# Two layers of attention and expert FFN on one core: who combines the expert results between the layers, and in which order the second layer's projections run

## The reference, cut to what matters

```python
x = x + _L0_xattn_ref(_layernorm(x), ctx_1024, ctx_1024, ...)   # 16 heads of 16, windows of 128 tokens
x = x + _L0_ffn_ref(_layernorm(x), ...)                         # 16 experts, 2 per token, and a shared one
x = x + _L1_xattn_ref(_layernorm(x), ctx_1024, ...)             # 16 heads of 16, 256 keys per query
x = x + _L1_ffn_ref(_layernorm(x), ...)                         # 8 experts, 2 per token

def _L0_ffn_ref(x, ...):
    logits = x @ router_w.T
    top_vals, top_idx = top_k(logits, 2)
    gates = sigmoid(top_vals)
    ...                              # every token: gates[0]*y_first + gates[1]*y_second + shared

def _L1_xattn_ref(q, kv, ...):
    qh, kh, vh = q @ Wq + bq, kv @ Wk + bk, kv @ Wv + bv
    attn = softmax(qh @ kh.T / sqrt(16))
    return (attn @ vh) @ Wo + bo
```

## Time and profile before

| | us |
|---|---|
| median of 3 runs | 889.52 (887.65 to 891.84) |
| the profiled execution | 891.48 |
| its span, first to last instruction | 889.7 |
| PE busy | 799.2 (90%) |
| DVE busy | 593.7 (67%) |
| ACT busy | 394.5 (44%) |
| GpSimd busy | 239.6 (27%) |

### The profile page before, as it was taken

The page is one execution under the profiler, slowest core; times in us unless marked ns, Lnnn a source line. Parts: engine busy times, 40 slices in busy tenths (PEclk is TensorE's granted clock), DMA queues, the critical chain, the costliest instruction groups (busy, mean ns, idle before and its releaser), DMA issues.

```text
span 889.7 us, 23526 instructions
## 1 busy us (share of the span) xinstructions
PE 799.2 (90%) x8688; PEld 595.3 (67%) x8689; DVE 593.7 (67%) x1394; ACT 394.5 (44%) x767; POOL 239.6 (27%) x201
## 2 busy tenths in 40 slices
PE   7998999898978888788979999989998999999993
PEld 4555666565667666666634666657487999999993
DVE  3456787789936555555966888856878755555552
ACT  3344556553412222223422666765776444444440
POOL 0004000100026666662003000001045644444442
PEclk8999999999989999999999999999999999999998
DMA  9886312234452222225845433128247333343331
GB/s 278 141 104 72 98 38 74 95 125 132 136 188 78 83 83 83 77 89 149 166 50 71 74 121 121 50 73 308 60 140 196 65 71 68 67 69 64 67 61 25
DMA packets 72345, 91.41 MB, mean 103 GB/s; under 512 B 14705, under 2 KB 57713, under 8 KB 72273
## 3 DMA queue, kind: packets, MB, share of 16 engines
q1 hardware_dynamic: 58112, 62.19, 29.3%
q0 software_dynamic: 13728, 27.94, 12.5%
q10 hardware_dynamic: 432, 0.26, 0.1%
HBM read 60.86 MB, written 17.56 MB: 88 GB/s over the span
## 4 chain that ended last, share of the span: by engine, by line
PE 62%; DVE 16%; issue 8%; ACT 5%; DMA 4%; another core or an unknown queue 2%; DVEq 1%; POOL 0%; SPq 0%; POOLq 0%; ACTq 0%
PE bank L1024 13%; PE bank L1011 12%; PE bank L763 5%; PE bank L783 3%; PE bank L918 3%; PE bank L729 3%; PE bank L578 3%; PE bank L609 3%; PE bank L559 2%; PE bank L930 2%; DMA out<-arena,put_i 2%; PE bank L996 2%; PE bank L596 2%; DVE arena L1850 2%
## 5 line engine op out<-in xcount | busy, mean ns | idle before, releaser
L1024 PE MATMUL bank<-arena 128*128 x1218 | 281.2, 274 | 6.8 <-DVE arena L1863 2.9
L1399 ACT ACTIVATE arena<-bank,router_b 128x128 f32<-128x128 f32 x312 | 87.4, 373 | 112.1 <-DMA router_b<-in_exp_b 97.3
L1556 DVE TENSOR_REDUCE neg_max<-bank 128x2 f32<-128x512 f32 (+1 forms) x180 | 117.3, 684 | 27.8 <-PE bank L729 27.5
L1024 PEld LDWEIGHTS bank<-arena 128*128 128x128 f16 x1218 | 119.2, 98 | 19.3 <-issue 17.3
L1011 PE MATMUL bank<-att,arena 128*128 128x128 f16 x960 | 106.2, 221 | 0.3 <-issue 0.3
L1237 ACT ACTIVATE arena<-bank 128x1024 f32<-128x1024 f32 x96 | 96.4, 1024 | 11.3 <-PE bank L748 11.2
L1011 PE MATMUL bank<-arena 128*128 128x128 f16 x1128 | 97.8, 223 | 2.4 <-issue 2.4
L1011 PE MATMUL bank<-attT,arena 128*128 128x128 f16 x912 | 99.3, 219 | 0.0
L1011 PEld LDWEIGHTS bank<-att,arena 128*128 x960 | 92.6, 99 | 6.4 <-issue 0.5
L2018 POOL DMA_INDIRECT out<-arena,put_i x39 | 67.3, 1725 | 107.4 <-DVE arena L1876 85.9
L1011 PEld LDWEIGHTS bank<-attT,arena 128*128 x912 | 86.6, 98 | 5.5
(11 more groups left out here) (223 smaller groups left out, 1349.4 us busy)
## 6 DMA issues: line engine op xcount, KB each, us to landing
arena<-arena SPq DMA_DIRECT2D x96, 128.0 KB, 5.2
arena<-in_exp_up SPq DMA_DIRECT2D x16, 512.0 KB, 3.9
arena<-in_exp_b SPq DMA_DIRECT2D x39, 128.0 KB
arena<-in_ctxT SPq DMA_DIRECT2D x8, 512.0 KB, 7.2
arena<-in_exp_dn SPq DMA_DIRECT2D x16, 256.0 KB, 4.2
xn_d<-arena POOLq DMA_DIRECT2D x8, 512.0 KB, 4.6
arena<-y_d SPq DMA_DIRECT2D x8, 512.0 KB, 8.9
arena<-in_exp_dn SPq DMA_DIRECT2D x4, 1024.0 KB, 5.5
```

Of the source, the lines that this page charges most:

```text
L1024: last = mm(yP[u], hidT[u][x][:, k], weights(e, 1, w, k * D, D), start=n == 0, stop=n == n_second - 1)
L1399: last = fn(hid[:, k * P:(k + 1) * P], upP[u][:, half, (k % 4) * P:(k % 4 + 1) * P], ACT.Relu, bias=b1_col[u][:, k:k + 1], scale=1 / WS)
L1556: v.tensor_reduce(neg_max[u][:, column(m * HM):column(m * HM) + 2 * HM - 1:2], mx[m % 2].rearrange("p (h k) -> p h k", h=HM), AX.X, ALU.ma ...
```

## The change

Five things, all in layer 1:

1. Chunks 2 and 3 are combined by GpSimd (`combine_late`): one product of 128x2048 numbers with the gates and two sums of 128x1024 for each chunk. DVE combines chunks 0 and 1 as before. GpSimd's bias sums no longer wait for all queries.
2. The keys of chunk 1 go to the bank `trT`, and so need no wait for the keys of chunk 0. The order of the products on PE, of the copies on ACT and of the steps on DVE is rewritten.
3. The eight first maxima follow directly behind the last turned chunk. The queries of chunk 3 are multiplied in four pieces between them (`last_queries`).
4. The values of chunk 3 are multiplied in four pieces between the maxima of tile 1 (`last_values`).
5. SP issues the stack DMAs of keys in another place: chunk 1's ahead of the load of the last expert results, chunks 2 and 3 inside `project`.

```diff
+        keysP = [[kP] * NC, [kP, trT, kP, kP]]
+        LATE = 2
...
@@ SP, project(1)
                     keys(1, 0)
                     load_results(2)
+                    keys(1, 1)
                     load_results(3)
-                    keys(1, 1)
+                    keys(1, 2)
                     queries(1, 0)
+                    keys(1, 3)
                     queries(1, 1)
+                    queries(1, 2)
...
@@ PE, keys, turn_tokens
-                    after(pe, s["kparts_ready"], c)
+                    if l == 0 or c > 1:
+                        after(pe, s["kparts_ready"], c - 1 if l and c == 2 else c)
...
+                    if l and c == 0:
+                        pe.wait_ge(s["kparts_ready"], 2)
...
@@ PE, project(1)
                     project_bias()
+                    keys(1)
                     pe.wait_ge(B[0]["y_ready"], NS[0])
                     values(0)
-                    keys(1)
+                    keys(2)
                     values(1)
-                    keys(2)
                     turn_tokens(0, 0)
-                    values(2)
                     queries(0, 0)
                     keys(3)
                     turn_tokens(1, 1)
-                    values(3)
+                    values(2)
                     queries(1, 1)
                     turn_tokens(2, 0)
                     queries(2, 0)
                     turn_tokens(3, 1)
-                    first_maxima(l, 0, 2)
-                    queries(NC - 1, 1)
-                    first_maxima(l, 2, 8)
+                    first_maxima(l, 0, 8)
                     turn_first(l)
...
+            def last_queries(n):
+                s, (m, k) = B[1], (n // KD, n % KD)
+                if n == 0:
+                    pe.wait_ge(s["qparts_ready"], NC - 1)
+                last = mm(qP[:, m], wqk[1][:, 0, k, m * P:(m + 1) * P], xnT[(NC - 1) % 2][:, k], start=k == 0, stop=k == KD - 1)
...
+            def last_values(t):
+                for k in range(KD):
+                    last = mm(vP[...], ctxT[...], wv[:, k], start=k == 0, stop=k == KD - 1)
...
@@ PE, first_maxima
-                    if l and m >= 2:
-                        if m == 2:
-                            pe.wait_ge(s["v_ready"], NC)
-                        keep_running(spare, 5 if m == 2 else 1, 3 * P if m == 2 else 2 * P)
+                    if l and 0 < m <= KD * KD:
+                        last_queries(m - 1)
+                    elif l and m:
+                        if m == KD * KD + 1:
+                            pe.wait_ge(s["kparts_ready"], NC)
+                        keep_running(kP[:, 0], 1, P)
...
@@ PE, maxima of tile 1
-                            if l == 0 and m == 2:
+                            if l and 0 < m <= TC:
+                                last_values(m - 1)
+                            elif l and m:
+                                keep_running(kP[:, 0], 1, P)
+                            elif m == 2:
...
@@ ACT, project(1)
                     keys(0)
                     output_bias()
+                    keys(1)
                     values(0)
-                    keys(1)
+                    keys(2)
                     root(0)
                     values(1)
-                    keys(2)
                     turned(0, 0)
+                    queries(0)
                     root(1)
-                    values(2)
-                    queries(0)
                     keys(3)
                     turned(1, 1)
                     root(2)
-                    values(3)
+                    values(2)
                     queries(1)
...
                     queries(3)
+                    values(3)
...
@@ DVE, prepare and project(1)
-                    if l:
+                    if l and c < LATE:
                         combine(0, c)
+                    elif l:
+                        dve.wait_ge(s["x_ffn"], (c - LATE + 1) * 3)
...
-                    prepare(0, 0, lambda: keys(1))
+                    keys(1)
+                    prepare(0, 0)
                     prepare(1, 1, lambda: keys(2))
-                    prepare(2, 0, lambda: queries(0))
+                    queries(0)
                     keys(3)
-                    prepare(3, 1, lambda: queries(1))
+                    prepare(2, 0)
+                    queries(1)
+                    prepare(3, 1)
                     queries(2)
-                    first_maxima(l, 0, 2)
+                    first_maxima(l, 0, 8)
+                    keep_first(l)
...
@@ GpSimd
+            def combine_late(c):
+                done = B[1]["x_ffn"]
+                pool.wait_ge(once["gates_ready"], 1)
+                pool.wait_ge(B[0]["gathered"][c % 2], (c // 2 + 1) * 2 * 16)
+                x = x_res[:, c * TC:(c + 1) * TC]
+                of = gates[:, c * TC:(c + 1) * TC].rearrange("p t i -> p i t").rearrange("p i (t o) -> p i t o", o=1)
+                n = 3 * (c - LATE)
+                pool.tensor_tensor(y_got[c], y_got[c], of.to_broadcast([P, 2, TC, D]), ALU.mult).then_inc(done, 1)
+                for i in range(2):
+                    pool.wait_ge(done, n + 1 + i)
+                    pool.tensor_tensor(x, x, y_got[c][:, i], ALU.add).then_inc(done, 1)
```

More of the change, by code:

```diff
@@ L670, in project @@
                     turn_tokens(3, 1)
-                    first_maxima(l, 0, 2)
-                    queries(NC - 1, 1)
-                    first_maxima(l, 2, 8)
+                    first_maxima(l, 0, 8)
                     turn_first(l)
+            def last_queries(n):
[3 more added lines that the diff above has]
+                last = mm(qP[:, m], wqk[1][:, 0, k, m * P:(m + 1) * P], xnT[(NC - 1) % 2][:, k], start=k == 0, stop=k == KD - 1)
+                if n == KD * KD - 1:
+                    last.then_inc(s["q_mm"], 1)
+            def last_values(t):
+                s, c = B[1], NC - 1
+                if t == 0:
+                    pe.wait_ge(s["v_ready"], c)
+                for k in range(KD):
+                    last = mm(vP[:, t // 2, (t % 2) * D:(t % 2 + 1) * D], ctxT[:, k, c * CW + t * P:c * CW + (t + 1) * P], wv[:, k],
+                              start=k == 0, stop=k == KD - 1)
+                if t == TC - 1:
+                    last.then_inc(s["v_mm"], 1)
             def first_maxima(l, lo, hi):
@@ L1133, in keys @@
                     for m in range(KD):
-                        last = fn(k_parts[c % 2][:, 0, m], kP[:, m], ACT.Identity, bias=bqk[:, 1, m:m + 1])
+                        last = fn(k_parts[c % 2][:, 0, m], keysP[l][c][:, m], ACT.Identity, bias=bqk[:, 1, m:m + 1])
                     last.then_inc(s["k_hi"], 1)
@@ L1487, in keys @@
                     dve.wait_ge(s["k_hi"], c + 1)
-                    cut_rest(k_parts[c % 2], kP, bqk[:, 1], s["kparts_ready"])
+                    cut_rest(k_parts[c % 2], keysP[l][c], bqk[:, 1], s["kparts_ready"])
                 def queries(c):
@@ L1973, in _ @@
                     pool.memset(v_all[:, :, :, HD:V1].rearrange("p t h o -> p (t h) o"), 1.0).then_inc(once["ones_set"], 1)
+                if l:
+                    for c in range(LATE, NC):
+                        combine_late(c)
                 pool.wait_ge(once["bias_step"], l * 5 + 4)
-                pool.wait_ge(s["qparts_ready"], NC)
+                if l == 0:
+                    pool.wait_ge(s["qparts_ready"], NC)
                 def add_bias(c, u):
```

16 lines of the change are left out of this document (4 added, 12 removed).

## The result

| us | before | after |
|---|---|---|
| median of the runs | 890.68 (4 runs, 887.65 to 892.33) | 905.03 (4 runs, 897.24 to 906.66) |
| profiled execution / its span | 891.48 / 889.7 | 906.03 / 904.2 |
| layer 0, up to the keys of chunk 0 | 407.44 | 409.14 |
| **the stretch**: from there to the first scores of layer 1 | 71.45 | 84.83 |
| behind the first scores | 410.8 | 410.2 |

The account below looks back on a forecast made before the run. PE, busy for 90% of the span, was taken to bound the kernel. Cost 3.0, gain 5.5 and cost 0.4 summed to -2.1 us, from the runs' median 889.52 to 887.4 us; range 884.0 to 895.0.

Parts of the forecast that it names:

- A rule that speaks against it: DVE combining chunk 1 beside GpSimd's product: two-input SBUF instructions contend, but DVE waits only once, to 436.7, costing nothing.
- cover: Slack behind DVE's combination of chunk 1, whose variance meets a root not free before 442.6; 3 us.
- rival 2: GpSimd and DVE take turns at the combination of chunk 1, ending about 454, not 436.3; about 901 us; chance 0.18.
- the one wait: DVE's combination of chunk 1 waits once for GpSimd's product, to 436.7, moving the variance from 439.7 to 443.1.
- The new wait on ACT: ACT's copy of keys 2 waits for a DMA ahead of the first root: chunk 0 5.6 us late, cost 3.0.
- The first maxima: On PE, eight maxima with four query pieces between them, up to tile 1: 8.5 us instead of 14.0, gain 5.5.
- tile 1's maxima: On PE, with pieces of chunk 3's values between them: 6.9 us and waits 0.2 instead of 6.7, cost 0.4.
- rival 4: PE's clock falls to half in the maxima without the fillers: 3.4 us more, 889 to 891 us; chance 0.06.
- GpSimd's own cost: GpSimd's combination of a chunk: product 4.7 us (2.35 to 7), each sum 2.35, together 9.6, hidden behind 4.6 us.
- there is little of a gap in which GpSimd could step in: Argument against turns at DVE's combination: its eight instructions take 3.38 us together, 0.42 from start to start.

Follow-up runs that it names:

- e5: The changed kernel with GpSimd's combination of chunks 2 and 3 left out and its bias sums behind all queries as before; ratio 1.0037, stretch 72.74 us.
- e4: The kernel before with only the first-maxima part of the change, and unread products of 128 columns between the other maxima; ratio 1.0033, stretch 71.05 us.
- e8: The kernel before with only the first-maxima part, unread products of 256 columns between later maxima and 384 ahead of the turn; ratio 1.0007, stretch 71.90 us.
- e1: The changed kernel, but GpSimd starts combining chunk 2 only after DVE has combined chunk 1; ratio 1.0147, stretch 84.82 us.
- e2: The changed kernel, but ACT does the root of chunk 0 ahead of its copy of the keys of chunk 2; ratio 1.0065, stretch 75.07 us.
- e9: The kernel before with only GpSimd's combination of chunks 2 and 3 and its early bias sums, old order and maxima kept; ratio 1.0078, stretch 78.00 us.

## Why the prediction was wrong

The failed step is the one in "A rule that speaks against it": "DVE waits once for the product ... I take this cover as sufficient". It was rival 2 that happened, to which I had given 0.18, at the place that it named and with a price near its own (about 901; measured 905). By the prediction's own numbers even the one wait used the cover up: it moves the variance of chunk 1 to 443.1, behind the root's 442.6. That the price is near is partly luck: rival 2 had all six of GpSimd's instructions hold the combination (17.7 us more) and a cost of 14 us; four did (10.8 us more), the cost was 9.1, and two things that it did not count, the sizes of the first two points and the half clock of the last, made up the rest.

Point by point, the stretch of the profiled executions:

- **The new wait on ACT.** The mechanism was right: the copy at 429.95 and the root at 432.52 (428.6 and 431.2 forecast, in a kernel whose layer 0 ends 1.7 us earlier), scaled chunk 0 in e5 6.1 us late (5.6 forecast), PE idle 5.23 (5.5), queries at half clock 6.01 (5.2). Up to the first maximum e5 needs 55.2 us and before 50.8: cost 4.4, forecast 3.0.
- **The first maxima.** Gain 4.3 us in e5, forecast 5.5. A piece with its maximum takes 1.38 us from start to start (473.85, then 475.22), where 0.32 and 0.86 were summed: the quarter of a group that runs in one piece costs 1.06 when it stands alone. The same holds for the pieces of the last values: tile 1's maxima take 8.1 us up to the scores in e5, 7.0 before: cost 1.1, forecast 0.4. (DVE's cut of queries 3 and its memset come ahead of them now, but PE does not wait for them in e5.) Together -3.2, forecast -5.1.
- **So without GpSimd** the change is +1.3 us in e5's profile, which is of its shortest execution, and about +3 by its ratio, not -2.1. This mis-sizing alone would have left the time inside the range.
- **GpSimd beside DVE.** Chunk 1 is scaled 47.3 us behind the start of the stretch in the changed kernel, 38.2 in e5: 9.1 us. The sum: combination 10.75, variance 1.28, scaling 1.53, minus 3.67 of cover (DVE's wait for ACT, 3.94 in e5, of which 0.27 is left) and 0.8 from an earlier start of DVE's, gives 9.1. Forecast: nothing.
- **Half clock in tile 1's maxima.** The last values take 2.07 us a piece instead of 1.13; from the keeping to the scores 11.2 us, in e5 8.1: 3.1 us. This is rival 4, at its price (3.4) and beside rival 2. Why the clock fell there is not shown; e4 and e8 have a fall at nearly the same place without GpSimd's part, and e5's profile has none.
- 1.3 + 9.1 + 3.1 is 13.5, and the stretch grew by 13.4.

GpSimd's own cost was over-estimated: the product took 3.65 to 3.86 us (4.7 forecast, 2.35 and 7 as ends). It did not matter.

What made me give rival 2 too little was the argument "there is little of a gap in which GpSimd could step in", from DVE's 0.42 us between starts. GpSimd got in with no larger gap than that: its product began at 435.55, while the fourth of DVE's eight ran, and the fifth was held. And I weighed the rule at one step of DVE's. The scaling and the variance stand in the same rows, within 10 us, and e1, e2 and e9 show that whichever of them is beside GpSimd pays.

## What to carry to other kernels

Before moving work from DVE to GpSimd, list DVE's instructions that will run in the same microseconds, and price each of the kinds that were held here (two tensors from the SBUF; a scaling by numbers per partition, SBUF to SBUF) at one whole instruction of GpSimd's, up to as many as GpSimd issues; a delay of GpSimd only picks which of them pays. If both must work, cut GpSimd's instructions short (4.67 us in place of 14.13 here), or place them beside steps that were not held (those that read PSUM, the statistics). Where one engine's list serves two chains, a DMA wait ahead of the first chain's short step (here the root, 0.2 us) delays all that waits for this step by the whole wait (6.1 us for chunk 0). And look at the clock of all executions, not only of the profiled one, before a stretch that got shorter is taken for a gain.

## What the runs showed of the hardware that was not expected

- The alternation was strict here, one instruction each, also with 0.48 us instructions against 3.8 us ones. Not held, in the changed kernel: the statistics (1.40 us for four at 449.76, beside sums of 448.20 to 453.02), `cut_rest`, which reads a bank (1.41 at 448.44, beside the same), and the reciprocal (0.18 at 453.33, beside a bias sum of 452.98 to 455.33).
- A tiny instruction is held too: the variance, 128x4 numbers, took 1.45 us instead of 0.17.
- GpSimd's product with a gate broadcast over 2048 numbers takes 3.6 us where it is held little or not (3.60 in e1 and e2), 1.8 for each 1024; its sum of two tensors 2.35 for each 1024.
- The 30.7 us at half clock in e4 and e8 went on while PE was busy 9.65 of 10 us (e8). A wait of 0.55 us stands right ahead of the fall; the rows show no more of a cause.
